# Latent attention: banks, order of TensorE, exponentials and shares of the value products

## The reference

```
c = h @ Wdkv
q, k, v = h @ Wq, c @ Wuk, c @ Wuv           # per head, 8 dimensions
scores = q @ k.T / sqrt(8)
scores = where(causal, scores, -1e9)
a = softmax(scores)
out = (a @ v).reshape(B, S, D) @ Wo
x = x + out
```

## Time and profile before

| | |
|---|---|
| median of three runs (lowest, highest) | 1059.56 us (1059.54, 1069.42) |
| profiled execution, span from first to last instruction | 1057.6 us |
| median of the runs less that span | 2.0 us |
| PE busy | 919.4 us, 87% |
| DVE busy | 785.7 us, 74% |
| ACT busy | 557.7 us, 53% |
| POOL busy | 490.0 us, 46% |
| DMA queues' share of 16 engines | 12.3% together |
| first score of the stage starts | 594.5 us |
| projection after its last mix starts | 792.7 us |

### The profile page before, as it was taken

The page is one execution under the profiler, slowest core; times in us unless marked ns, Lnnn a source line. Parts: engine busy times, 40 slices in busy tenths (PEclk is TensorE's granted clock), DMA queues, the critical chain, the costliest instruction groups (busy, mean ns, idle before and its releaser), DMA issues.

```text
span 1057.6 us, 19542 instructions
## 1 busy us (share of the span) xinstructions
PE 919.4 (87%) x6337; PEld 655.6 (62%) x6337; DVE 785.7 (74%) x2080; ACT 557.7 (53%) x1494; POOL 490.0 (46%) x451
## 2 busy tenths in 40 slices
PE   6898985888778999869997598988989999989987
PEld 4787533767578989727775243434437677768774
DVE  6889999999756777769998376777734744589982
ACT  4675456886444445724443156766764233445533
POOL 5444553555066564635556777574530600024430
PEclk9999896999879999969999659989999999999998
DMA  9300000000111111410000322222102000000001
GB/s 324 149 1 1 2 6 1 1 1 1 41 39 39 41 40 33 109 66 1 0 1 0 107 67 62 82 76 62 31 1 101 1 1 1 1 2 2 1 1 40
DMA packets 29828, 40.55 MB, mean 38 GB/s; under 512 B 11468, under 2 KB 25036, under 8 KB 29228
## 3 DMA queue, kind: packets, MB, share of 16 engines
q1 hardware_dynamic: 27244, 34.28, 10.3%
q0 software_dynamic: 2496, 5.16, 1.9%
HBM read 31.44 MB, written 7.82 MB: 37 GB/s over the span
## 4 chain that ended last, share of the span: by engine, by line
PE 27%; issue 14%; POOL 7%; DVE 5%; ACT 3%; SPq 1%; DMA 0%; DVEq 0%; POOLq 0%; ACTq 0%
POOL att L1787 6%; PE ps L1163 4%; PE ps L829 4%; PE ps L1135 4%; PE ps L819 4%; PE ps L1147 3%; PE ps L793 1%; PE ps L1249 1%; PE ps L1257 1%; DVE rs L2124 1%; PE ps L1101 1%; DVE stats L2001 0%; SPq L570 0%; PE ps L1106 0%; DVE U L2029 0%
## 5 line engine op out<-in xcount | busy, mean ns | idle before, releaser
L1787 POOL TENSOR_TENSOR att<-att,ri 128x1232 f32<-128x1232 f32 x64 | 169.3, 2645 | 190.5 <-DVE ri L2130 190.5
L793 PE MATMUL ps<-VW,PT 128*128 128x128 f32 (+3 forms) x1280 | 157.6, 278 | 17.5 <-DVE x L2145 16.0
L793 PEld LDWEIGHTS ps<-VW,PT 128*128 128x128 f32 (+1 forms) x1280 | 148.4, 192 | 35.2 <-DVE x L2145 28.3
L1369 ACT ACTIVATE PT<-ps 128x512 f32<-128x512 f32 x128 | 70.6, 594 | 89.5 <-PE ps L766 88.7
L766 PE MATMUL ps<-W,att 128*128 128x128 f32 (+1 forms) x640 | 86.9, 282 | 16.2 <-POOL att L1787 14.7
L1761 POOL TENSOR_TENSOR rstd<-ve,minus_half 128x4 f32<-128x4 f32 x38 | 38.8, 1039 | 114.2 <-DVE ve L2016 97.7
L900 PE MATMUL ps<-PT,att 128*128 128x128 f32 x624 | 80.8, 285 | 8.5 <-issue 8.4
L829 PEld LDWEIGHTS ps<-U,att 128*128 128x128 f32 x512 | 66.3, 191 | 33.1 <-issue 29.1
L766 PEld LDWEIGHTS ps<-W,att 128*128 128x128 f32 (+1 forms) x640 | 72.7, 143 | 22.3 <-POOL att L1787 15.5
L2581 DVE CUSTOM_DVE_ANT_0 C<-ps,cmaskb 128x512 bf16<-128x512 f32 (+1 forms) x128 | 71.1, 555 | 20.7 <-PE ps L1135 18.0
L2581 DVE CUSTOM_DVE_ANT_0 U<-ps,cmaskb 128x384 bf16<-128x384 f32 (+1 forms) x128 | 53.9, 421 | 41.8 <-PE ps L1135 41.5
(11 more groups left out here) (432 smaller groups left out, 2105.6 us busy)
## 6 DMA issues: line engine op xcount, KB each, us to landing
U<-in_ffn SPq DMA_DIRECT2D x1, 6176.0 KB, 23.2
U<-split SPq DMA_DIRECT2D x144, 32.0 KB
W<-split SPq DMA_DIRECT2D x144, 32.0 KB
W<-in_packed SPq DMA_DIRECT2D x1, 2162.5 KB, 23.5
U<-in_ffn SPq DMA_DIRECT2D x1, 2060.0 KB, 9.7
U<-in_moe SPq DMA_DIRECT2D x1, 2048.0 KB, 7.3
split<-VBD SPq DMA_DIRECT2D x4, 384.0 KB, 2.9
split<-W SPq DMA_DIRECT2D x4, 384.0 KB, 2.7
```

Source lines behind the costliest of these rows:

```text
L793: q = mm(attended(s, t), PT[0:m, t.slot(2), c, :], batch(VW, t.group)[0:m, c * D:(c + 1) * D], start=(c == 0), stop=(c == NC - 1))
L1369: go(PT[:, t.slot(2), 4 * k:4 * k + 4, :].rearrange("p c n -> p (c n)"), ps[:, k0 + k, :], ACT.Copy).then_inc(probsT, 1)
L1787: tt(p, p, over_keys(ri[:, t.slot(2), :]), ALU.mult).then_inc(probs, 1)
```

## The change

Four things change together.

Banks: score 0 has bank 0, score 1 has bank 2, scores 2 and 3 lie side by side in bank 4. By key, blocks 0 and 1 have banks 1 and 3, and blocks 3 and 2 lie side by side in bank 5. A product waits for the reader of its own bank in the step before. The maxima of scores 2 and 3 wait until both are written.

Order of TensorE in a step: score 0 of k+8, score by key 0 of k, the value product of k-5, score 1, score by key 1, the extra, scores 2 and 3, scores by key 3 and 2.

Exponentials: one instruction of 384 columns takes blocks 3 and 2, so there are three for each step. The exponentials lie in another order in SBUF (PROB_AT), and the select of the diagonal blocks becomes two instructions, of three blocks and of one. ScalarE's copy of bank 6 comes one step earlier, at k = 12 + 8u behind exponential 1.

Value products: the 1280 columns of a quad are cut into four shares of 320. Share 0 is one piece of key block 0; share 1 is 192 columns of block 0 and 128 of block 1; share 2 is 256 of block 1 and 64 of block 2; share 3 is 192 of block 2 and 128 of block 3.

```diff
--- before.py
+++ after.py
@@ -91,7 +91,13 @@
 UNITS, QUADS, WAYS = 2 * B, 4 * B, 4
 LEAD = 8
 LAG = 5
-RINGS = 3
+SCORE_BANK = (0, 2, 4, 4)
+SCORE_AT = (0, 0, 0, 2 * P)
+KEY_BANK = (1, 3, 5, 5)
+KEY_AT = (0, 0, P, 0)
+PROB_AT = (0, S, 2 * S, S + 3 * P)
+EXPS = 3
+SHARES_OF_QUAD = (((0, 0, 320),), ((0, 320, S), (1, P, 2 * P)), ((1, 2 * P, S), (2, 2 * P, 320)), ((2, 320, S), (3, 3 * P, S)))
 HOLD = 4
 SIGNS = 96
 STACK = PIECES * PIECES * HD
@@ -1131,20 +1137,20 @@
                 t, i = WAYS * step + way, TB - 1 - way
                 if g == 0 and way == 0:
                     pe.wait_ge(stacked[n % HOLD], 16 * 2 * PIECES * PIECES * (n // HOLD + 1))
-                wait(pe, qk_max, t - RINGS + 1)
-                mm(ps[:, 2 * (t % RINGS), 0:(i + 1) * P], queries[0:STACK, n % HOLD, g, i * P:(i + 1) * P],
+                wait(pe, qk_max, WAYS * (step - 1) + max(way + 1, WAYS * (way // 2)))
+                z, at = (i + 1) * P, SCORE_AT[way]
+                mm(ps[:, SCORE_BANK[way], at:at + z], queries[0:STACK, n % HOLD, g, i * P:(i + 1) * P],
                    keys[0:STACK, n % HOLD, g, 0:(i + 1) * P], start=True, stop=True).then_inc(qk_ps, 1)
 
             def score_by_key(step, j):
 
 
                 n, g = divmod(step, WAYS)
-                t = WAYS * step + j
                 if g == 0 and j == 0:
                     pe.wait_ge(neg_set, n + 1)
-                wait(pe, kq_exp, t - RINGS + 1)
-                rows = SIGNS + PIECES * WAYS
-                mm(ps[:, 2 * (t % RINGS) + 1, 0:S - j * P], keys[0:rows, n % HOLD, g, j * P:(j + 1) * P],
+                wait(pe, kq_exp, EXPS * (step - 1) + min(j, 2) + 1)
+                rows, at = SIGNS + PIECES * WAYS, KEY_AT[j]
+                mm(ps[:, KEY_BANK[j], at:at + S - j * P], keys[0:rows, n % HOLD, g, j * P:(j + 1) * P],
                    queries[0:rows, n % HOLD, g, j * P:S], start=True, stop=True).then_inc(kq_ps, 1)
 
             def weigh(n, j):
@@ -1157,12 +1163,14 @@
                         pe.wait_ge(extra_read, read("values", b))
                     if m == 0:
                         wait(pe, oT_sb, u)
-                    pe.wait_ge(diag_set, WAYS * (n + 1))
-                for g in range(WAYS):
-                    at = j * VROW + (4 * c + g) * 4 * VE + m * 2 * VE
-                    t = mm(ps[32 * g:32 * g + 32, 6, j * P:S], held_at[b % 2][:, at:at + 32],
-                           probabilities(n, g)[:, j * S:j * S + S - j * P],
-                           start=(m == 0 and j == 0), stop=(m == 1 and j == TB - 1))
+                    pe.wait_ge(diag_set, 2 * WAYS * (n + 1))
+                for block, a, z in SHARES_OF_QUAD[j]:
+                    for g in range(WAYS):
+                        at = block * VROW + (4 * c + g) * 4 * VE + m * 2 * VE
+                        first = PROB_AT[block] - block * P
+                        t = mm(ps[32 * g:32 * g + 32, 6, a:z], held_at[b % 2][:, at:at + 32],
+                               probabilities(n, g)[:, first + a:first + z],
+                               start=(m == 0 and block == 0 and a == 0), stop=(m == 1 and block == TB - 1))
                 if j == TB - 1:
                     t.then_inc(pv_ps, 1)
 
@@ -1170,23 +1178,23 @@
                 ahead, now = 0 <= k + LEAD < TB * QUADS, 0 <= k < TB * QUADS
                 if ahead:
                     score(k + LEAD, 0)
-                    score(k + LEAD, 1)
-                if 0 <= k - 1 < TB * QUADS:
-                    score_by_key(k - 1, TB - 1)
-                if ahead:
-                    score(k + LEAD, 2)
                 if now:
                     score_by_key(k, 0)
-                    score_by_key(k, 1)
                 if 0 <= k - LAG < TB * QUADS:
                     weigh(*divmod(k - LAG, TB))
+                if ahead:
+                    score(k + LEAD, 1)
+                if now:
+                    score_by_key(k, 1)
                 if extra(k) is not None:
                     beside(*extra(k))
                 if k in (16 * B + 7, 16 * B + 8):
                     keys_values(X3, k - 16 * B - 7)
                 if ahead:
+                    score(k + LEAD, 2)
                     score(k + LEAD, 3)
                 if now:
+                    score_by_key(k, 3)
                     score_by_key(k, 2)
 
             pe.wait_ge(ld["moe"], 32)
@@ -1668,29 +1676,27 @@
 
             def exponent(step, j):
                 n, g = divmod(step, WAYS)
-                t = WAYS * step + j
                 if g == 0 and j == 0:
                     wait(act, pv_ps, n - 1)
-                act.wait_ge(kq_ps, t + 1)
-                go(probabilities(n, g)[:, j * S:j * S + S - j * P], ps[:, 2 * (t % RINGS) + 1, 0:S - j * P], ACT.Exp)\
-                    .then_inc(kq_exp, 1)
+                act.wait_ge(kq_ps, WAYS * step + (j + 1 if j < 2 else WAYS))
+                at, z = (PROB_AT[j], S - j * P) if j < 2 else (PROB_AT[3], 3 * P)
+                go(probabilities(n, g)[:, at:at + z], ps[:, KEY_BANK[j], 0:z], ACT.Exp).then_inc(kq_exp, 1)
 
             for k in STEPS:
-                if k >= 13 and (k - 13) % 8 == 0 and (k - 13) // 8 < UNITS:
-                    u = (k - 13) // 8
+                now = 0 <= k < TB * QUADS
+                if now:
+                    exponent(k, 0)
+                    exponent(k, 1)
+                if k >= 12 and (k - 12) % 8 == 0 and (k - 12) // 8 < UNITS:
+                    u = (k - 12) // 8
                     act.wait_ge(pv_ps, 2 * u + 2)
                     if u >= 1:
                         act.wait_ge(extra_ps, put("out", u - 1))
                     go(oT, ps[:, 6, :], ACT.Copy).then_inc(oT_sb, 1)
-                now = 0 <= k < TB * QUADS
-                if now:
-                    exponent(k, 0)
-                    exponent(k, 1)
                 if extra(k) is not None:
                     beside(*extra(k))
                 if now:
                     exponent(k, 2)
-                    exponent(k, 3)
                 if k == 60:
                     gate_exp_moe(0)
                 if k in (16 * B + 7, 16 * B + 9):
@@ -1936,7 +1942,7 @@
             def spread(n):
 
 
-                wait(pool, diag_set, WAYS * n - 2)
+                wait(pool, diag_set, 2 * (WAYS * n - 2))
                 pool.wait_ge(extra_read, read("turn", n))
                 rows = slice(SIGNS, SIGNS + PIECES * WAYS)
                 pool.tensor_copy(queries[rows, n % HOLD, :, :],
@@ -1944,10 +1950,12 @@
                 pool.wait_ge(neg_set, n + 1)
 
             def hide_later_keys(n, g):
-                pool.wait_ge(kq_exp, WAYS * (WAYS * n + g + 1))
-                diag = probabilities(n, g).rearrange("p (c n) -> p c n", n=P)[:, 0:PROB // P:TB, :]
-                pool.affine_select(diag, diag, [[0, TB], [1, P]], ALU.is_ge, 0.0, base=0, channel_multiplier=-1)\
-                    .then_inc(diag_set, 1)
+                pool.wait_ge(kq_exp, EXPS * (WAYS * n + g + 1))
+                blocks = probabilities(n, g).rearrange("p (c n) -> p c n", n=P)
+                for first, last in ((0, 3 * TB), (PROB_AT[3] // P, PROB_AT[3] // P + 1)):
+                    diag = blocks[:, first:last:TB, :]
+                    pool.affine_select(diag, diag, [[0, -(-(last - first) // TB)], [1, P]], ALU.is_ge, 0.0, base=0,
+                                       channel_multiplier=-1).then_inc(diag_set, 1)
 
             for k in STEPS:
                 n, rest = divmod(k + 4, 4)
@@ -2575,10 +2583,10 @@
                 t, i = WAYS * step + way, TB - 1 - way
                 if g == 0 and way == 0:
                     wait(dve, nm_split, n - 1)
-                dve.wait_ge(qk_ps, t + 1)
+                dve.wait_ge(qk_ps, WAYS * step + max(way + 1, WAYS * (way // 2)))
                 wait(dve, qk_max, t - 1)
-                z = (i + 1) * P
-                v.tensor_tensor_reduce(unused[t % 2][:, 0:z], ps[:, 2 * (t % RINGS), 0:z], visible[:, S - z:S], -1.0, -NEG,
+                z, at = (i + 1) * P, SCORE_AT[way]
+                v.tensor_tensor_reduce(unused[t % 2][:, 0:z], ps[:, SCORE_BANK[way], at:at + z], visible[:, S - z:S], -1.0, -NEG,
                                        ALU.add, ALU.min, nm[:, n % 2, g, i:i + 1]).then_inc(qk_max, 1)
 
             def beside(name, n):
```

## The result

Over 20 runs of each, the changed kernel has a median of 1058.47 us (1050.40 to 1062.25) and the kernel before 1063.31 us (1055.42 to 1069.42): ratio 0.9950, 95% interval 0.9933 to 0.9967. So it is faster by half a percent, -5.3 us (-3.5 to -7.1), within the 1% of my forecast. The forecast of 1058 met the absolute time partly by luck: its base, the three runs first shown, lay 3.8 us under the median of 20. The change that I forecast, 1.6 us from that base (2.2 from the profile), is less than the smallest gain that the interval allows.

What follows compares the result with a forecast made beforehand. TensorE's columns, with its clock and small waits, and GpSimd's splitting in two stretches bound the stage; -7.9 + 3.8 + 2.5 + 1.7 + 1.2 + 0.5 - 1 - 3 = -2.2 us, median 1057.4, stated 1058; range 1046 to 1070.

Steps and rivals of the forecast that it cites:

- GpSimd's stretches: Keys extra to product, steps 12-17 and 28-33: GpSimd's splitting chain bounds both; +2.5 us in all, shrinking would prove it wrong.
- the price of the second select: GpSimd's select split into 384 + 128: about 0.25 us more per pair (bounds 0 and 0.64).
- one new drop: TensorE's clock falls anew after the longer idle wait at step 17: +1.7 us.
- Small waits: TensorE outside GpSimd's two stretches, clock loss taken off: 12.1 us lost, 7.9 removed by banks and order, 4.2 kept.
- VectorE's hold behind the write at step 43: An addition and statistics hold VectorE after the write, so a TensorE wait stays: 1.5 us kept.
- The added switches: TensorE, outside GpSimd's stretches: each of 27 extras brings one more switch of 0.1 us (bounds 0 and 0.2), 2.7 us.
- Product pieces: TensorE's value products, seven pieces for four: 0.1 us per four steps (bounds 0 and 0.45).
- The third rival: Each added value-product piece pays two loads of 0.11 us: 6.9 us over 42 steps, total 1065 us; chance 0.06.
- the slack of the select: Every fourth product needs its unit's last select: 1.1 us slack vanishes where no extra pads, 0.3 us in four places, 1.2.
- The ends: Stage's start (594-626) gains 1 us (bounds 0, 2); its end (771-794) gains 3 (bounds 0, 4).
- The first: Only TensorE's need stays outside GpSimd's stretches, no new clock drop or kept waits: 1045 to 1047 us; chance 0.21.
- The second: The product waits for the select in every unit, 13 times 0.9 us, plus more clock drops: 1072 us; chance 0.17.

Runs made afterwards that it cites:

- experiment 3: Changed kernel with the value products as four whole blocks again (512, 384, 256, 128 columns): 1063.12 us, 0.9988 to the kernel before.
- experiment 4: Kernel before with the value products in equal shares of 320 columns alone: 1066.12 us, ratio 1.0007 to the kernel before.
- experiment 6: Changed kernel with the select first in GpSimd's step and whole blocks as shares: 1045.21 us, 0.9852 to the kernel before.
- experiment 5: Changed kernel with GpSimd's select of the step before moved ahead of both splits, nothing else: 1046.99 us, 0.9849 to the kernel before.
- experiment 8: Changed kernel with the value product 0.33 us later, behind score 1 and score by key 1: 1051.70 us, 0.9896 to the kernel before.
- experiment 11: Kernel before with the select of the four diagonal blocks as two instructions, three blocks and one: 1066.53 us, 1.0034 to the kernel before.

## Why the prediction was right, and where it was not

**The sum.** I forecast -2.2 us for the stage against the profiled execution; the profiles give -2.0. That agreement is luck, twice over: the measured gain is 5.3 us, and the sum is made of terms that were off in both directions. What was right is that columns and GpSimd's work don't shrink, so that little is gained.

**GpSimd's stretches.** The mechanism was right: they hold, with 4.3 us waits. From the keys extra to the product the first went from 15.2 to 15.8 us and the second from 17.1 to 16.8, where I had +1.25 each. A stretch that shrinks was my own sign of being wrong, and the second did, by 0.3 us. The reason is a reading that I missed: in the kernel before GpSimd did not run without a gap from 689.89, since its select at 696.11 waited 0.84 us for ScalarE, as this line of its timeline shows:

```profile
696.11 0.65 POOL L1949 TENSOR_SCALAR_AFFINE_SELECT KBD<-KBD 128x512 f32<-128x512 f32 x1 [0.84 <-ACT KBD L1675]
```

In the changed kernel that gap is gone. Without it both chains grew by some 0.5 us, four selects of 0.13 us more (0.77 less 0.64). So the price of the second select was too high: I took 0.25 from a short cast, and forecast 0.85 to 0.9 for the pair.

**The clock.** The step that failed most in size. I took one new drop at 1.7 us. Behind the product of step 17 the clock was low for 7.8 us (0.87 over 30) where it had been full. In the stretch behind step 33 it was low for 15.6 (0.88 over 65) where before it was 6.6: by the finer windows some 8.3 behind the select's wait, where it was 3.4, and 6.9 behind VectorE's wait at step 43, where it was 3.4. By my own rule of half of it that is 3.9 and 4.5 us lost more, 8.4 in place of 1.7, and some 1.7 of it has nothing to do with the select.

**Small waits.** I forecast 12.1 us of them, 7.9 to go and 4.2 to stay. On TensorE's products themselves, all waits but those for the select sum to 8.2 us before (steps 5 to 57) and to 2.6 after, so 5.6 went; shorter gaps are not in that list. The copy of the sums stopped TensorE nowhere in the changed kernel's list (kept: 1.6 us). VectorE's hold behind the write at step 43 did stay, 1.7 us (kept: 1.5). Loads still waited 10.4 us for VectorE, not under 5 as I wrote, but little of it stops the score products: 2.3 us, where before it was 3.9 of 18.2. The added switches I took at 2.7 us have no row of their own in any run, and stay open.

**Product pieces.** 0.01 us each at most, against 0.1 per four steps. The third rival fails: with it each two-piece share would have cost 0.22 us more, and 758.65 to 759.34 is 0.69 us, as the single piece is with 0.68. So the rule of the Trainium skill, TensorE: Matmul & The Clock Gate, part 3, that a weight load overlaps running products only where the row groups differ, does not hold for these tiles; the measurement decides.

**Equal shares.** A step that may have failed: I costed them as added pieces only (0.1 us per four steps), and had the slack of the select in another paragraph without joining the two. Experiments 3, 4 and 6 suggest that the changed kernel needs the 0.3 us that they put ahead of the product; the profiles don't confirm the size, as said there.

**The ends.** -1 and -3 expected. From the first score to the product of step 5 it went from 31.9 to 29.2 us, 2.7 less and outside the bounds of 0 to 2; part of it may be the clock, 0.68 there where it was 0.50, but in experiment 3, with 0.50 throughout, the stretch took 29.9. From the product of step 57 to the last projection it went from 22.2 to 20.1.

**The rivals.** The first, all small waits go and no clock drop, comes near what happens once the select is early: it was priced at 1045 to 1047, and experiment 5 measured 1046.99. Part of that match is chance, since the price stands on the same low base, and experiment 5 got there by other terms: it has a slow spell at step 43, and its two GpSimd stretches are 2.0 and 2.6 us shorter than the rival left them. The second, a wait for the select in every unit, is there with 0.2 to 1.2 us in seven places beside the two long waits, far from its 0.9 us in 13.

## What to carry to other kernels

When a change takes waits away from the busiest engine, ask which other engine's chain that engine reaches next, and what stands in that engine's own queue ahead of the one instruction that is waited for. Here moving a single call in GpSimd's loop, with no work added, gave about 1% on top of the change, twice what the whole change gave; on the kernel before, where the two waits were 1.5 and 1.0 us, it gave 0.5%. A wait of 4 us on TensorE is to be priced with the slow clock behind it, where here about as much again was lost. And a single profile per kernel is not enough to price a gain of half a percent: the stage differed by 2.0 us between the profiles here, and the kernels by 5.3.

## What the runs showed of the hardware

In the changed kernel TensorE's granted clock fell to 1.2 GHz during the waits of 4.3 us and stayed there for some 8 us after each, although the engine was busy for all 8.0 us of the first (0.53 from 663 to 671) and 8.97 of 9 us of the second (0.54 from 710 to 719). Shorter waits gave no steady price. In experiment 5 no spell followed the select's waits of 1.15 and 1.16 us. Behind VectorE's wait at step 43, of 1.7 us in both, the clock was low for 6.8 us in the changed kernel and in experiment 5, and not at all in experiment 8. In experiment 11 a wait of 1.98 us stands at the start of a slow spell of 13.7 us.

A value product of 320 columns costs 0.68 us in one piece, 0.69 in two of 192 and 128 columns and 0.68 in two of 256 and 64, to the same 32-column tiles. A GpSimd select of three blocks and one of a single block, back to back, take 0.77 us against 0.64 for one of four blocks.
